# A router stage on VectorE: one maximum pass instead of four, the eight best logits found one slot later, and a count table written by ScalarE

## The reference, cut to what matters

```
logits = x @ router_weight.T                     # 2048 tokens x 64 experts
probs  = softmax(logits)
topw, topi = top_k(probs, 8)
topw   = topw / sum(topw)
oh     = one_hot(topi.reshape(-1), 64)
pos    = cumsum(oh)[..] - 1                      # place of a token in its expert's list, kept if < 256
```

## Time and profile before

| what | value |
| --- | --- |
| median of 3 runs | 1306.81 us |
| the profiled execution's own time | 1304.94 us |
| its span, first to last instruction | 1303.1 us |
| VectorE busy | 1126.7 us (86%) |
| TensorE busy | 1127.9 us (87%) |
| GpSimd busy | 952.4 us (73%) |
| ScalarE busy | 845.0 us (65%) |

### The profile page before, as it was taken

The page is one execution under the profiler, slowest core; times in us unless marked ns, Lnnn a source line. Parts: engine busy times, 40 slices in busy tenths (PEclk is TensorE's granted clock), DMA queues, the critical chain, the costliest instruction groups (busy, mean ns, idle before and its releaser), DMA issues. The chain is left out here.

```text
span 1303.1 us, 19362 instructions
## 1 busy us (share of the span) xinstructions
PE 1127.9 (87%) x6421; PEld 751.0 (58%) x6421; DVE 1126.7 (86%) x1571; ACT 845.0 (65%) x1520; POOL 952.4 (73%) x747
## 2 busy tenths in 40 slices
PE   6789998889998889797786669999999999999950
PEld 2333434434443533344333359899999999999940
DVE  4689999889999799998899849988889899898847
ACT  5765567635757346675444358888888888888833
POOL 0798668968899798799798235777777777777644
PEclk9788998799878979997895869999999999999985
DMA  8338324441255232523222348999999999999988
GB/s 312 75 81 273 79 73 98 134 99 34 67 130 146 49 86 51 144 63 117 53 52 88 105 141 241 309 304 302 303 307 304 307 308 307 304 307 299 291 136 333
DMA packets 95138, 235.03 MB, mean 180 GB/s; under 512 B 18608, under 2 KB 18864, under 8 KB 94400
## 3 DMA queue, kind: packets, MB, share of 16 engines
q1 hardware_dynamic: 64320, 162.44, 41.2%
q0 software_dynamic: 30720, 71.36, 22.9%
HBM read 147.33 MB, written 52.85 MB: 154 GB/s over the span
## 5 line engine op out<-in xcount | busy, mean ns | idle before, releaser
L1148 POOL TENSOR_TENSOR dbu<-rep,bc 128x1024 f32<-128x1024 f32 x128 | 301.8, 2362 | 61.5 <-DVE hst L1322 29.3
L1322 DVE TENSOR_TENSOR_SCAN hst<-hst,dbu 128x512 f32<-128x512 f32 x256 | 298.9, 1213 | 37.0 <-POOL dbu L1148 25.3
L1817 POOL DMA_INDIRECT sum_rows<-ye,tokens x128 | 205.4, 1605 | 99.2 <-issue 51.8
L418 PE MATMUL y_ps<-dbu,cs 128*32 128x512 f32 x512 | 156.1, 693 | 75.2 <-DVE dbu L1328 47.6
L883 ACT ACTIVATE hst<-rep,small_sb 128x512 f32<-128x512 f32 x256 | 165.8, 684 | 62.3 <-DVE dbu L1328 61.9
L1809 POOL DMA_INDIRECT xe<-x_rows,tokens x128 | 151.6, 1184 | 67.4 <-issue 37.8
L456 PE MATMUL ring<-first_raw,xT 128*128 128x512 f32 x384 | 183.1, 623 | 1.9 <-ACT made L905 1.9
L1328 DVE TENSOR_TENSOR dbu<-hst,bc 128x1024 f32<-128x1024 f32 x128 | 156.7, 1224 | 4.4
L1859 PE MATMUL low<-xh,w1h 128*128 128x256 f32 x512 | 150.5, 294 | 0.0
L1859 PE MATMUL low<-xl,w1h 128*128 128x256 f32 x512 | 145.2, 284 | 0.0
L1859 PE MATMUL low<-xh,w1l 128*128 128x256 f32 x512 | 145.2, 284 | 0.0
(11 more groups left out here) (217 smaller groups left out, 2672.1 us busy)
## 6 DMA issues: line engine op xcount, KB each, us to landing
first_raw<-in_gate_up SPq DMA_DIRECT2D x64, 768.0 KB
rep<-made SPq DMA_DIRECT2D x256, 128.0 KB
second_raw<-in_down SPq DMA_DIRECT2D x64, 256.0 KB
bc<-bc_rows SPq DMA_DIRECT2D x64, 128.0 KB, 3.2
second_raw<-in_down SPq DMA_DIRECT2D x64, 128.0 KB
rows<-sum_rows SPq DMA_DIRECT2D x16, 512.0 KB, 9.6
sum_rows<-x2T SPq DMA_DIRECT2D x1, 4608.0 KB, 16.8
xT<-in_x_turned SPq DMA_DIRECT2D x16, 256.0 KB
```

The costliest lines, as they stand in the source:

```text
L418: ins = pe.matmul(y_ps[rows, :], sel, dbu[:, n % WORK, g, :], start=(k == 0), stop=(k == QUADS - 1))
L1148: pool.tensor_tensor(dbu[:, n % WORK, :, :], rep[:, i % 2, :, 1, :], bc[:, k, 0, :].unsqueeze(1).broadcast_to([P, 2, T]), ALU.mult).then_i ...
L1322: dve.tensor_tensor_scan(h, h, dbu[:, n % WORK, i, :], 0.0, ALU.mult, ALU.add).then_inc(scanned, 1)
L1817: pool.indirect_dma_start(sum_dram[e % SUMS], bass.IndirectOffsetOnAxis(ap=tokens[:, e, j:j + 1], axis=0), ye[:, e % YE, j, :], None, comp ...
```

## The change

In the three windows `shift_logits` takes the plain maximum of each token by one reduction and subtracts it; the eight largest are then found by MAX8 in the shifted logits one slot later, at the head of `choose`, and a new semaphore `nearest` tells ScalarE, whose `exponents` waits for that instead of the freed bank. The weights (sum, reciprocal, product) become `weigh`, which runs after slot 6, ahead of `find_slots`. The count table is written by ScalarE after its decays of slot 6 in the third window (`spread_counts`). In the last batch the same instructions stand in the same order, except that the table comes from ScalarE.

```diff
-ROUTE_STEPS = 22
-PLACE_STEPS = 24
+ROUTE_STEPS = 18
+PLACE_STEPS = 20
...
+            def spread_counts():
+                full(act, f"dt{B - 1}_{MI - 1}")
+                act.activation(count8, cs[:, C_COUNT:C_COUNT + P].unsqueeze(2).broadcast_to([P, P, TOPK]), ACT.Copy)\
+                    .then_inc(counted, 1)
...
             def exponents(b):
                 if b < B - 1:
-                    taken(act, f"logits{b}")
+                    act.wait_ge(nearest, b + 1)
...
+                    if c == 1 and last:
+                        spread_counts()
...
-                for j in range(NT):
-                    own.step(dve.max(top[:, j, :], logits[:, j, :]))
+                own.step(dve.tensor_reduce(small[:, 0, :], logits, AX.X, ALU.max))
                 own.settle()
-                own.step(dve.tensor_tensor(near[:, :, :], top[:, :, :], top[:, :, 0].unsqueeze(2).broadcast_to([P, NT, TOPK]),
-                                           ALU.subtract))
-                dve.tensor_tensor(lsm[:, :, :], logits, each(top[:, :, 0]), ALU.subtract).then_inc(drain_sem(f"logits{b}"), 1)
+                dve.tensor_tensor(lsm[:, :, :], logits, each(small[:, 0, :]), ALU.subtract).then_inc(drain_sem(f"logits{b}"), 1)
...
                 if b < B - 1:
-                    own.settle()
                     taken(dve, f"logits{b}")
+                    for j in range(NT):
+                        ins = dve.max(near[:, j, :], lsm[:, j, :])
+                    ins.then_inc(nearest, 1)
+                    dve.wait_ge(nearest, b + 1)
...
                 dve.tensor_scalar(chose[:, :, :], mask[:, :, :], 0.0, None, ALU.is_gt).then_inc(masked, 1)
+
+            def weigh(b, own):
                 dve.wait_ge(exped, b + 1)
...
             def number_slots(b, own):
-                if b == B - 2:
-                    full(dve, f"dt{B - 1}_{MI - 1}")
-                    dve.tensor_copy(count8, cs[:, C_COUNT:C_COUNT + P].unsqueeze(2).broadcast_to([P, P, TOPK]))
...
             def number_tokens(j):
                 dve.wait_ge(placed, 1)
+                dve.wait_ge(counted, 1)
...
                     if back and c == 1:
+                        weigh(b - 1, chain["route"])
                         find_slots(b - 1, chain["route"])
...
             choose(B - 1, chain["route"])
+            weigh(B - 1, chain["route"])
```

More of the change, by code:

```diff
@@ L324, in mixers @@
         shifted = sem("shifted")
+        nearest = sem("nearest")
+        counted = sem("counted")
         exped = sem("exped")
```

## The result

The changed kernel took 1303.14 us (median of 17 runs), the kernel before 1307.52 (17 runs beside them). The ratio is 0.9959 (95% interval 0.9939 to 0.9979), about 5.4 us less (2.7 to 8.0 by the interval; the two medians differ by 4.4). The forecast was 8.2 less, 1298.6 us, with a range of 1293.5 to 1307.0. A second measurement gave 0.9967 (0.9939 to 0.9995). The sign was right, and so was the mechanism inside the windows; the size was some 1.5 times too large, at the edge of what the interval allows. Yet the two profiled executions have almost the same span: 1303.0 us after, 1303.1 before. Why the total says less than the windows is part of the story.

What follows compares the result with a forecast made beforehand. VectorE was taken as the bound up to 740 us, with TensorE's chain from the logits' bank setting slot 6 in the windows. Slot 6 gains of 11.86 less 3.65 of delays gave -8.2: 1298.6 us, range 1293.5 to 1307.0.

Steps and rivals of the forecast that it cites:

- The bank freed earlier: In the windows one PSUM reduction replaces four MAX8 and L1429; the logits' bank is free 1.27, 2.42 and 3.65 us earlier.
- The clock: TensorE's sum of squares with q and k takes 7.99 us in all three windows: 4.52 us more gained.
- Slots 4 and 5: VectorE's work there stays even, a held mask adds 0; slot 6 comes 1.27, 4.11 and 6.48 us earlier, 11.86 together.
- The moved weights: After slot 6 GpSimd's multiplies hold them on VectorE: slot 7 is 1.75 us late in window 1, 3.7 in the others.
- After slot 7 and the table: Shorter holds and no cast on VectorE, table hidden on ScalarE: delays of 1.75, 1.3 and 0.6 us remain, 3.65 together.
- the sum against the time: Last step: -11.86 + 3.65 = -8.2 us, all taken off the profiled 1304.94 us, giving 1296.7; the median lies 1.87 higher.
- The sign of being wrong: Wrong if slot 6 comes early and slot 8 does not, or if the windows' gain is gone by 740 us.
- The clock falls anyway: Rival, chance 0.15: TensorE's clock still falls in the windows, the 4.52 us are missing, 1303.1 us.
- No hold: Rival, chance 0.2: the moved product stays at 0.42 us, or L1478 gets in ahead of slot 8's multiply; 1294.8 us.
- More holds than counted: Rival, chance 0.11: VectorE's two-SBUF operations after the windows are held, 2.37 us each; with six more, 1312.8 us.
- Priced at nothing: TensorE waits longer for slot 7 in the windows and its clock may fall sooner: taken as 0, at most 1 us each.

Runs made afterwards that it cites:

- Experiment e: Kernel before, with TensorE computing part of q once more for nothing while it waits for the logits' bank in windows 2 and 3: 1304.04 us, ratio 0.9973.
- h: Changed kernel with the reciprocals in unused columns of a PSUM bank, so the moved product reads one SBUF and one PSUM tile: 1301.01 us, ratio 0.9944.
- c: Kernel before with only the count table moved to ScalarE in the third window: 1310.80 us, ratio 1.0033; measured again 1310.84 us, 1.0020.
- a: Kernel before with only the plain maximum, the eight found a slot later; weights and table as before: 1302.19 us, ratio 0.9953.
- d: Changed kernel with the weights put back right behind the mask, after slot 4: 1301.42 us, ratio 0.9958.
- b: Kernel before with only the weights moved from after slot 4 to after slot 6: 1315.59 us, ratio 1.0056.
- i: d with the mask of the eight made by ScalarE instead of VectorE in the windows: 1299.70 us, ratio 0.9939.

## Why the prediction was right, and where its size was off

- **The bank freed earlier.** Forecast 0.44 + 0.41 = 0.85 after the arrival; measured 612.60 - 611.73 = 0.87. The reduction took 0.42, next to its lower bound.
- **The clock.** Forecast 7.99 us for the two groups in every window; measured 8.00 (window 3: 612.75 to 620.75). Experiment e isolates the term.
- **Slots 4 and 5.** Slot 6 at 10.41 in windows 1 and 2: gains of 1.25 and 4.08 for 1.27 and 4.11. In window 3 it was 5.56 for 6.48: the mask was held for 2.0 us, the case that I had priced at up to 2.4 and set to 0, because the next hold would absorb it. It did: slot 8 came where it was forecast. h shows the same from the other side: there the mask took 0.48 us, slot 6 came at 10.41, and slot 8 still at 26.37.
- **The moved weights.** Forecast: in windows 2 and 3 the product held to the end of slot 7's multiply and the sum into prev to that of slot 8; in window 1 the product held to the end of both, and the sum free. All so in the changed kernel's first profile: the product took 2.64, 1.65 and 0.92 us, the sum 0.23, 1.96 and 1.98 (the prediction had over 2 for the last two).
- **After slot 7 and the table.** The first operation behind slot 7 in window 2 (L1487, held for 2.63 us in the earlier trace rows; L1498 in the changed kernel) took 0.28, and the table's cast was gone. The three windows together: -8.2 us forecast, 86.4 - 78.2 = 8.2 measured. One by one they are +0.58, -2.90 and -5.85 for +0.48, -2.8 and -5.9.
- **The step that was mis-sized is the last one, the sum against the time.** The prediction put the stretches between the windows at 0 ("I take 0, at most 1 a window") and took the whole gain of the windows off the time. From the first logits to slot 112 the changed kernel needs 374.7, 369.1 and 374.5 us, the kernel before 378.4 and 377.8: 5.3 less on the mean, next to the measured 5.4, and only 3.6 less in the first pair. In two of three profiles the stretches between the windows took 4.5 and 4.4 us more than in the first profile of the kernel before.
- **Long windows in one profile do not explain it.** In the second profile of the kernel before the logits came 1.1 and 1.6 us later against GpSimd's product in windows 2 and 3, L1429 took 1.15 and 1.97 us instead of 2.29 and 3.52, and slot 6 came at 11.66 and 14.19 us (against 14.49 and 16.87). But the whole way was only 0.6 shorter, and the three profiles of c, whose code is the same up to there, have slot 6 of windows 2 and 3 at 14.5 and 16.9 like the first profile. Five profiles of the two kernels are few, and the interval of the time is wide: how much the changed kernel loses between the windows, and whether the change is the reason, stays open.
- **The sign of being wrong that was nearly met** is "the gain of the windows is gone by 740 us": in the first pair slot 124 came 4.1 us earlier (707.74 against 711.87), the first gather only 1.2 (759.45 against 760.67).
- **Slips in the sums.** The own range of 1295.5 to 1303 doesn't follow from its terms: +0.5, +3 and 2.4 each way around 1298.6 give 1296.2 to 1304.5. Four more holds cost 9.5 us, which is 1.3 more than the gain of 8.2 and does not leave 1.3 of it; five make the kernel 3.7 slower, under the 3.9 that the prediction itself calls 0.3%.
- **The rivals.** "The clock falls anyway" is refuted: the two groups took 8.0 us in all three windows of every profile of a kernel with the new maximum. "No hold" came true once in nine cases: in the second profile of the changed kernel, window 1, the product slipped in between two multiplies of GpSimd, took 0.43 and pushed the second one back (the pair took 4.94 us for 4.67 in the first profile): 23.91 for 25.46 us. "More holds than counted" did not come behind the third window: from slot 112 to 124 it is 69.5 or 69.6 us in every profile.
- **Priced at nothing.** TensorE's slow stretch behind slot 7 is there (idle 3.0 to 5.3 us, in window 3 then 0.55 of the full clock from 636 to 647 us), and cost nothing that the windows or the 69.5 us show. Nor is it what lengthens the first stretch between windows. That one took 148.6, 147.1 and 148.5 us in the changed kernel, 146.6 and 146.9 before and 146.9 in a and d, whose weights stand early; but b, whose weights stand late and whose TensorE idles as long there (4.37 us), has the shortest of all, 145.5.

## What to carry to other kernels

An operation held inside an engine counts as busy; find it by a length that doesn't fit its size, and by its end falling just behind the end of another engine's instruction (0.1 to 0.3 us here). Not only operations with two SBUF inputs were held: the mask (2.03 us) and the cast have one. Taking such an operation off the list of a waiting engine pays twice, by the wait and by TensorE's clock behind it; but moving another operation with two SBUF inputs under the same multiplies gives part of it back, and freeing one only hands the hold to the next. A window is no measure by itself when its start moves too: read a stretch that holds all the windows and what lies between them, in more than one profile, before taking a gain off the time.

## What was not expected of the hardware

The Trainium skill (SBUF — State Buffer, section "Who interferes with whom") says that of a VectorE operation with two SBUF inputs and a GpSimd operation that reads SBUF, the one issued first goes first. By the starts in the profile these rows do not agree with that: six operations that stand ahead of the multiply in the profile were held to its end all the same. They are the cast (638.66, multiply at 638.89), L1487 (461.72, multiply at 461.94), the first operation behind slot 7 in c (639.26, multiply at 639.48), the sum into prev in d (626.07, multiply at 626.18) and in i (626.13, multiply at 626.86), and the key's product in h (452.74, multiply at 453.35). In each GpSimd was just issuing an indirect DMA ahead of the multiply. The sum into prev in h, 0.75 us ahead (452.60), was not held (0.23 us). So the order of starts in the profile is no safe sign of who waits within about 0.7 us; what the engines did inside these 0.7 us no row shows.

The other is the clock in window 1 of the kernel before: behind the same 1.34 us of idle time q and k took 7.11 us in the earlier trace rows and 8.81 in the second profile. One idle time does not decide the clock of what follows.

```profile
266.29 1.02 PE L516 MATMUL ring<-ones,rot 128*128 128x1 f32 x8 [1.34 <-DVE x2T L1431]
267.17 8.81 PE L456 MATMUL ring<-first_raw,xT 128*128 128x512 f32 x16
```
